# Looked-up ids broadcast by DMA as 16-bit halves, a shorter GpSimd clear between gathers, and constants built between the first gathers

## The reference, cut to what matters

```python
e = jnp.stack([tbl_0[ids[:, 0]], tbl_1[ids[:, 1]], ..., tbl_38[ids[:, 38]]], axis=1)   # (512, 39, 32)
p = e[:, ROW, :]                                  # ROW, COL: all i < j
q = e[:, COL, :]
z = jnp.einsum('bpc,apc,bpa->bp', p, w, q)        # (512, 741)
h = jnp.concatenate([z, dense_ctx], axis=1)       # (512, 757)
h = jnp.maximum(h @ W_top1 + b_top1, 0.0)         # 512 wide
h = jnp.maximum(h @ W_top2 + b_top2, 0.0)         # 256 wide
y = h @ W_top3
```

## Time and profile before

| | us |
|---|---|
| median of 3 runs | 199.92 (199.55 to 202.13) |
| profiled execution, own time | 198.71 |
| its span | 197.0 |
| TensorE matmul busy | 184.5 (94%) |
| VectorE busy | 144.1 (73%) |
| GpSimd busy | 135.4 (69%) |
| ScalarE busy | 42.7 (22%) |

### The profile page before, as it was taken

The page is one execution under the profiler, slowest core; times in us unless marked ns, Lnnn a source line. Parts: engine busy times, 40 slices in busy tenths (PEclk is TensorE's granted clock), DMA queues, the critical chain, the costliest instruction groups (busy, mean ns, idle before and its releaser), DMA issues.

```text
span 197.0 us, 3278 instructions
## 1 busy us (share of the span) xinstructions
PE 184.5 (94%) x1320; PEld 64.4 (33%) x1320; DVE 144.1 (73%) x137; ACT 42.7 (22%) x64; POOL 135.4 (69%) x202
## 2 busy tenths in 40 slices
PE   6999988969999999999999999799989976999895
PEld 3534533332222222322322222223322212222782
DVE  4889998965899989976663999589664349747600
ACT  4956941030001100111112100110121111210722
POOL 7988899888888888888888888888922200440000
PEclk9999999999999999999999999999999999999999
DMA  6999940000000100000000000000000000000000
GB/s 166 278 290 419 387 138 15 10 17 12 10 13 10 20 10 12 12 14 13 10 13 14 11 13 10 15 13 15 12 0 3 0 0 0 0 5 0 0 0 0
DMA packets 6688, 9.75 MB, mean 49 GB/s; under 512 B 1977, under 2 KB 4477, under 8 KB 6673
## 3 DMA queue, kind: packets, MB, share of 16 engines
q1 hardware_dynamic: 3696, 8.00, 12.6%
q0 software_dynamic: 2944, 1.51, 4.4%
q10 hardware_dynamic: 32, 0.03, 0.1%
HBM read 9.53 MB, written 0.00 MB: 48 GB/s over the span
## 4 chain that ended last, share of the span: by engine, by line
POOL 55%; PE 32%; issue 7%; DVE 2%; DMA 1%; ACT 1%; DVEq 0%; POOLq 0%
POOL gathered L395 41%; POOL pause L402 13%; PE ps L609 10%; PE ps L623 10%; PE ps L634 6%; PE ps L654 4%; PE ps L646 2%; DVE prod L518 2%; DMA gathered<-tbl,ids_sb 1%; POOL sel L384 1%; PE ps L587 1%; PE ps L663 0%; ACT eT L448 0%; POOL sel L387 0%; ACT z_sb L455 0%
## 5 line engine op out<-in xcount | busy, mean ns | idle before, releaser
L518 DVE TENSOR_TENSOR prod<-ps,eT 128x1024 f32<-128x1024 f32 (+2 forms) x91 | 110.2, 1265 | 36.2 <-PE ps L609 31.6
L395 POOL DMA_INDIRECT gathered<-tbl,ids_sb x92 | 92.3, 1003 | 15.2 <-issue 15.0
L609 PE MATMUL ps<-eT,w_sb 32*128 32x512 f32 (+2 forms) x380 | 70.7, 640 | 4.4 <-DVE prod L518 2.9
L623 PE MATMUL ps<-prod,sel 128*32 128x512 f32 x380 | 51.5, 604 | 0.0
L609 PEld LDWEIGHTS ps<-eT,w_sb 32*128 32x128 f32 (+2 forms) x380 | 22.0, 183 | 52.0 <-issue 25.1
L402 POOL MEMSET pause<- 128x256 f32 x91 | 30.3, 333 | 0.1
L503 DVE TENSOR_SCALAR hot<-ids_half,row_of 125x2048 bf16<-125x2048 f16 x34 | 27.8, 881 | 1.5 <-PE ps L576 0.9
L409 POOL TENSOR_TENSOR tabs<-tabs 128x512 f32<-128x512 f32 x8 | 10.1, 1264 | 25.0 <-ACT tabs L469 25.0
L576 PE MATMUL ps<-hot,lower 125*32 125x512 bf16 x272 | 22.0, 401 | 0.0
L634 PE MATMUL ps<-z_sb,w_sb 128*128 128x512 f32 x40 | 20.4, 624 | 0.7 <-ACT eT L448 0.7
L623 PEld LDWEIGHTS ps<-prod,sel 128*32 128x32 f32 x380 | 8.1, 108 | 33.7 <-issue 21.0
(11 more groups left out here) (36 smaller groups left out, 63.5 us busy)
## 6 DMA issues: line engine op xcount, KB each, us to landing
w_sb<-w SPq DMA_DIRECT2D x1, 1536.0 KB
gathered<-tbl,ids_sb POOLq DMA_INDIRECT x92, 2.3
tabs<-hot SPq DMA_DIRECT2D x3, 448.0 KB
w_sb<-wst SPq DMA_DIRECT2D x1, 640.0 KB, 13.1
w_sb<-wst SPq DMA_DIRECT2D x1, 576.0 KB, 12.0
tabs<-hot SPq DMA_DIRECT2D x1, 560.0 KB
w_sb<-wst SPq DMA_DIRECT2D x1, 512.0 KB, 10.5
w_sb<-w SPq DMA_DIRECT2D x1, 512.0 KB
```

The source lines that it names most:

```text
L395: pool.indirect_dma_start(gathered[J][:, b, K * r:K * r + K], None, tables[f], bass.IndirectOffsetOnAxis(ap=ids_sb[:, F * b + f:F * b + f ...
L518: dve.tensor_tensor(prod[:, x:x + n, :], ps[:, s:s + n, :], eT[:, I:I + 1, :].broadcast_to([P, n, B]), ALU.mult).then_inc(multiplied, 1)
L609: mm = pe.matmul(ps[:, RUN_BANK[p] + i - first, :], w_sb[rows, w_tile(q), :], eT[rows, J, :], start=True, stop=True)
L623: mm = pe.matmul(z_ps[K * (u % G):K * (u % G) + K, :], sel[:, u // G, :], prod[:, RUN_SLOT[p] + t - FIRST_TILE[p], :], start=(u < G), stop ...
```

## The change

**The ids** of the looked-up fields are handed over as 16-bit integers, one row of 2048 for each group. Four DMAs with a repeated source row bring them straight to 125 partitions: group 0 from ScalarE's queue as its first instruction, groups 1, 2 and 3 from SyncE's queue, each ahead of table 1, of table 2, and of the pair matrices of block 0. Everything of the old way goes: the int32 load, the f16 cast, `spread`, the 16 products, the copies from PSUM. `ids_half` is now unsigned 16-bit.

**GpSimd** makes the row numbers, waits for the ids and issues its first gather. The five steps that make the identity and `sel` stand behind gathers 1 to 5 in place of clears; from the sixth on the clear is 128x128.

**TensorE** starts with 14 products of zeros of 128x128x512 in bf16 on bank 7, and none later. The look-ups have banks of their own (4 and 5 for group 2).

**ScalarE** makes the lower tables of group 0 in two pieces of four slices, and TensorE waits for each piece. In the plan "lower" 1, 2 and 3 stand behind the look-ups of the group before; each still stands ahead of that group's "keep" on ScalarE.

```diff
-PAUSE = 256
-WARM = [2, 2]
+PAUSE = 128
+WARM = 14
+LOWER_PIECES = [[(0, 4), (4, 8)], [(0, 8)], [(0, 8)], [(0, 10)]]
...
-    steps += [("ids", 0), ("lower", 0), ("ids", 1), ("hot", 0, 0, 8), ("look", 0, 0, 3), ("lower", 1), ("ids", 2),
-              ("look", 0, 3, 8), ("keep", 0), ("lower", 2), ("ids", 3), ("hot", 1, 0, 8), ("look", 1, 0, 8),
-              ("lower", 3), ("keep", 1), ("hot", 2, 0, 8), ("look", 2, 0, 8), ("keep", 2), ("hot", 3, 0, 4),
+    steps += [("lower", 0), ("hot", 0, 0, 8), ("look", 0, 0, 8), ("lower", 1), ("keep", 0), ("hot", 1, 0, 8),
+              ("look", 1, 0, 8), ("lower", 2), ("keep", 1), ("hot", 2, 0, 8), ("look", 2, 0, 8), ("lower", 3),
+              ("keep", 2), ("hot", 3, 0, 4),
...
-        ids_half = [sb(f"ids_half{h}", [P, G, B], F16) for h in range(NHOT)]
+        ids_half = [sb(f"ids_half{h}", [P, G, B], U16) for h in range(NHOT)]
...
-        look_ps = [[ps[:, bank, :] for bank in banks] for banks in [(0, 1), (2, 3), (0, 1), (6, 7)]]
-        ids_ps = [ps[0:HP, bank:bank + G, :] for bank in (0, 4, 4, 4)]
+        look_ps = [[ps[:, bank, :] for bank in banks] for banks in [(0, 1), (2, 3), (4, 5), (6, 7)]]
...
+            def load_hot_ids(h):
+                sp.dma_start(ids_half[h][0:HP, :, :].rearrange("p f b -> p (f b)"),
+                             hot_ids[h:h + 1, :].broadcast_to([HP, G * B])).then_inc(hot_ids_in[h], 16)
+
             sp.dma_start(ids_sb[:, :], ids).then_inc(ids_in, 16)
             load_table(0)
+            load_hot_ids(1)
             load_table(1)
+            load_hot_ids(2)
             load_table(2)
+            load_hot_ids(3)
             for J in range(3):
                 load_w(J)
             load_table(3)
...
-            pauses = 0
+            gathers = pauses = 0
...
-                    if pauses:
-                        pool.wait_ge(paused, pauses)
-                    if (J, r, b) != (*fields[-1], NCHUNK - 1):
+                    gathers += 1
+
+                    if gathers == 1:
+                        pool.memset(ident[:, :], 0.0).then_inc(consts_zero, 1)
+                    elif gathers == 2:
+                        pool.wait_ge(consts_zero, 1)
+                        pool.affine_select(out=ident[:, :], in_=ident[:, :], compare_op=ALU.not_equal, fill=1.0,
+                                           base=0, pattern=[[-1, P]], channel_multiplier=1).then_inc(consts_made, 1)
+                    elif gathers == 3:
+                        pool.memset(sel[:, :, :], 1.0).then_inc(consts_zero, 1)
+                    elif gathers == 4:
...
+                    elif gathers < NCHUNK * len(fields):
+                        if pauses:
+                            pool.wait_ge(paused, pauses)
                         pool.memset(pause[:, :], 0.0).then_inc(paused, 1)
                         pauses += 1
...
-            act.dma_start(hot_ids_sb[:, :], hot_ids).then_inc(hot_ids_in, 16)
-            act.wait_ge(hot_ids_in, 16)
-            act.activation(ids16[:, :], hot_ids_sb[:, :], ACT.Copy).then_inc(ids16_made, 1)
+            act.dma_start(ids_half[0][0:HP, :, :].rearrange("p f b -> p (f b)"),
+                          hot_ids[0:1, :].broadcast_to([HP, G * B])).then_inc(hot_ids_in[0], 16)
...
                     act.wait_ge(tab_in[h], 16 * len(tab_pieces))
-                    for i in range(2):
-                        act.activation(lower[i][h][0:HP, :, :], bytes_of[h][0:HP, :, 1 - i::4], ACT.Copy,
-                                       scale=256.0 if i == 0 else 1.0).then_inc(lower_made, 1)
+                    for a, b in LOWER_PIECES[h]:
+                        for i in range(2):
+                            act.activation(lower[i][h][0:HP, :, K * a:K * b],
+                                           bytes_of[h][0:HP, :, 4 * K * a + 1 - i:4 * K * b:4], ACT.Copy,
+                                           scale=256.0 if i == 0 else 1.0).then_inc(lower_made, 1)
...
-            dve.memset(prod[0:K, 0, :], 0.0).then_inc(warm_zeroed, 1)
-            dve.wait_ge(consts_made, 1)
-            dve.tensor_copy(spread[:, :, :], ident[0:NHOT * G, 0:NHOT * G].rearrange("p (f o) -> p f o", o=1)
-                            .broadcast_to([NHOT * G, NHOT * G, HP])).then_inc(spread_made, 1)
+            dve.memset(prod[:, 0, :], 0.0).then_inc(warm_zeroed, 1)
...
-            keep_warm(2, WARM[0])
-            pe.wait_ge(ids16_made, 1)
-            pe.wait_ge(spread_made, 1)
+            zeros = prod[:, 0, :].bitcast(BF16)
+            for _ in range(WARM):
+                pe.matmul(ps[:, 7, :], zeros[:, 0:P], zeros[:, 0:B], start=True, stop=True)
...
-                        pe.wait_ge(lower_made, 2 * (h + 1))
-                        if h == 2:
-                            pe.wait_ge(eT_made, turns(LOOKED[0]))
                     for c in range(c0, c1):
                         n = SLICE_BASE[h] + c
+                        if any(c == a for a, _ in LOWER_PIECES[h]):
+                            pe.wait_ge(lower_made, lowers_of(h, c))
                         pe.wait_ge(hot_made, n + 1)
...
-    arrays["hot_ids"] = np.ascontiguousarray(a["ids"].T[[f for fields in HOT_FIELDS for f in fields]])
+    arrays["hot_ids"] = np.ascontiguousarray(np.ascontiguousarray(a["ids"].T).view(np.uint16)[:, ::2]
+                                             [[f for fields in HOT_FIELDS for f in fields]].reshape(NHOT, -1))
```

More of the change, by code:

```diff
@@ L10 @@
 BF16 = mybir.dt.bfloat16
-F16 = mybir.dt.float16
 F32 = mybir.dt.float32
@@ L207, in turns, with lowers_of @@
     return TURNS.index(J) + 1
-def halves_of(h):
-    return h + 2
+def lowers_of(h, c):
+    return 2 * (sum(len(pieces) for pieces in LOWER_PIECES[:h]) + 1 + [a <= c < b for a, b in LOWER_PIECES[h]].index(True))
 def lay_out_weights(w, W_top1):
@@ L286, in dlrm_tower @@
         ids_in = sem("ids_in")
-        hot_ids_in = sem("hot_ids_in")
+        hot_ids_in = [sem(f"hot_ids_in{h}") for h in range(NHOT)]
         tab_in = [sem(f"tab_in{h}") for h in range(NHOT)]
@@ L420, in _ @@
             for step in PLAN:
-                if step[0] == "ids":
-                    h = step[1]
-                    if h == 0:
-                        for part in (slice(0, 2), slice(3, 4)):
-                            act.wait_ge(ids_spread, part.stop)
-                            act.activation(ids_half[h][0:HP, part, :], ids_ps[h][:, part, :],
-                                           ACT.Copy).then_inc(ids_half_made, 1)
-                    else:
-                        act.wait_ge(ids_spread, G * (h + 1))
-                        act.activation(ids_half[h][0:HP, :, :], ids_ps[h], ACT.Copy).then_inc(ids_half_made, 1)
-                elif step[0] == "lower":
+                if step[0] == "lower":
                     h = step[1]
                     act.wait_ge(tab_in[h], 16 * len(tab_pieces))
-                    for i in range(2):
-                        act.activation(lower[i][h][0:HP, :, :], bytes_of[h][0:HP, :, 1 - i::4], ACT.Copy,
-                                       scale=256.0 if i == 0 else 1.0).then_inc(lower_made, 1)
+                    for a, b in LOWER_PIECES[h]:
[3 more added lines that the diff above has]
+                                           scale=256.0 if i == 0 else 1.0).then_inc(lower_made, 1)
                 elif step[0] == "keep":
@@ L461, in _ @@
                         act.wait_ge(mlp_in, 16 * len(mlp_loads))
-                        act.wait_ge(lower_made, 2 * NHOT)
+                        act.wait_ge(lower_made, lowers_of(NHOT - 1, NSLICE[-1] - 1))
                         act.wait_ge(hot_used, len(hot_block))
@@ L536, in side_free @@
                     pe.wait_ge(*side_used.pop())
-            def keep_warm(bank, n):
-                zeros = prod[0:K, 0, :]
-                for _ in range(n):
-                    pe.matmul(ps[:, bank, 0:B // 2], zeros[:, 0:P], zeros[:, 0:B // 2], start=True, stop=True)
             pe.wait_ge(warm_zeroed, 1)
-            keep_warm(2, WARM[0])
-            pe.wait_ge(ids16_made, 1)
-            pe.wait_ge(spread_made, 1)
+            zeros = prod[:, 0, :].bitcast(BF16)
+            for _ in range(WARM):
+                pe.matmul(ps[:, 7, :], zeros[:, 0:P], zeros[:, 0:B], start=True, stop=True)
             for step in PLAN:
-                if step[0] == "ids":
-                    h = step[1]
-                    if h > 1:
-                        pe.wait_ge(ids_half_made, halves_of(h - 1))
-                    for r in range(G):
-                        pe.matmul(ids_ps[h][:, r, :], spread[:, G * h + r, :], ids16[:, :],
-                                  start=True, stop=True).then_inc(ids_spread, 1)
-                    if h == 1:
-                        pe.wait_ge(third_made, 1)
-                        pe.wait_ge(ids_half_made, halves_of(0))
-                        keep_warm(2, WARM[1])
-                elif step[0] == "look":
+                if step[0] == "look":
                     h, c0, c1 = step[1:]
```

33 lines of the change are left out of this document (9 added, 24 removed).

## The result

The changed kernel takes **209.28 us** (median of 4 runs, 206.87 to 209.89) where the kernel before takes 199.85 us (199.55 to 202.13): ratio 1.042, 95% interval 1.031 to 1.054. The forecast was 199.1 us, range 194.2 to 203.2. The profiled execution took 209.85 us with a span of 208.1 us, against 197.0 before.

A forecast was written before the change was run, and what follows sets the result against it. TensorE's list and the front that starts it were taken as the bound, GpSimd's gathers being worth only 1.34 us. Front shift +0.5 less 1.34 gave -0.8 us, from a median of 199.92 to 199.1 us, range 194.2 to 203.2.

The forecast's parts named there:

- The bound and the stall: TensorE's list sets the time once begun; its one wait for block 8's gathered rows goes with the shorter clear, -1.34 us.
- The comparisons: VectorE's look-up slices wait for GpSimd's clear; the shorter one gives 0.77 us a slice from 0.835, bounds 0.835 and 0.66.
- The slow form for unsigned ids: Rival, chance 0.03: unsigned 16-bit ids cost VectorE's comparisons their fast form, +15 us, 214 us.
- The ids' arrival: Group 0's ids land at 9.75 us: 1.9 plus 50 rows at 0.157 us on five DMA engines; 12.8 at 0.218.
- divisor rule: A DMA uses the largest number of engines up to 16 dividing its rows, so 125 rows run on five.
- The cold start: TensorE stands still before the look-ups and may begin them at the low clock: 0.5 us charged, bounds 0 and 2.
- At no cost ... the other groups' ids: Id loads of groups 1 and 2 land near 11.4 and 17 us at 0.157 us per row, before use, costing nothing.
- 1.9 + 141p: Landing time of table 3 behind the id broadcasts, p us per row; above p = 0.189 ScalarE's keep 2 must wait.
- The gathers' ids: Row ids for GpSimd's gathers share engines with the broadcast: 1 us later at most, covered by 6 us of slack.
- Table 3 behind the backlog: Rival, chance 0.10: table 3 lands late behind the id loads and holds up ScalarE's keep 2, +4.9, 204.8 us.
- the ids did not come early: Rival, chance 0.27, claimed early ids: group 0's at 5.5 us, first multiplication at 27.2, total -5.5, 194.4 us.
- the comparisons did gain: Rival, chance 0.10, claimed no gain: the clear does not disturb the comparisons, slices stay at 0.835 us, +1.0, 200.9 us.

The follow-up runs named there:

- experiment 2: Changed kernel with each id load going to 128 partitions: 197.51 us, ratio 0.973; with the old clear of 256 columns as well: 204.36 us, ratio 1.020.
- experiment 5: Changed kernel with id loads split 112 and 13, gathers' ids first, constants before the gathers: 196.39 us with clear 128, 199.79 us with clear 256.
- experiment 3(b): Changed kernel with only group 0's id load on 128 partitions, the others at 125: 294.26 us on a chip where VectorE is held up; table 3 lands at 35.5.

## Why the prediction was wrong, step by step

- **The bound and the stall.** Right that a shift of the first multiplication passes through to the end, to 0.1 us in the table above, and GpSimd's period past 45 us is 1.33 us (1.32 forecast). That the wait for block 8's rows is gone is in part luck. Its last gather starts 2.9 us earlier and not some 8, since the first gather is 1.6 us later and the clears beside the comparisons grew; the rows land near 122.7 us (120.28 + 2.4), not by 119. TensorE did not wait because its own front was late: with the front mended and the same clear it waits twice, 1.5 us in all (experiment 2). The wait is gone where the gathers also start early, at 3.17 us (experiment 5).
- **The comparisons.** Quicker, as forecast, but by a wrong mechanism. I took the comparison to wait for the clear, and 0.77 us a slice; 22 slices took 15.49 us, 0.704 each, inside the bound of 0.66. The slow form for unsigned ids is out with it. It is the clear that waits, as the groups of 14 to 26 us show (count, busy us and mean ns, idle before), and then all clears with min/median/max in ns:

```profile
L494 DVE TENSOR_SCALAR hot<-ids_half,row_of 125x2048 bf16<-125x2048 uint16 x19 | 13.1, 765 | 0.0
...
L408 POOL MEMSET pause<- 128x128 f32 x6 | 4.0, 671 | 0.0
```

```profile
L408 POOL MEMSET pause<- x86: 218/219/696, 15.1 to 135.9; 128x128 f32 x86
```

  Before, one comparison in two stretched to 1.12 us beside a clear of 0.326; now none does, and the clear takes 0.671 us instead of 0.218. GpSimd's period there is 2.03 us, where 1.202 + 0.205 + 0.165 would be 1.57. It cost nothing here; in experiment 2 it and the late first gather together leave the 1.5 us of waits. The Trainium skill's page "SBUF — State Buffer" (section "Who interferes with whom") says that the shared port pair is an exclusive lock and that issue order decides who blocks; these rows agree.
- **The ids' arrival.** 10.96 us against 9.75. The five engines fit: 128 rows or a split bring 6.0 to 6.4 us, and from 10.5 to 11.0 us the DMA share is 0.32, where five of sixteen are 0.31. The row cost (10.96 - 1.9) / 50 = 0.181 us, between my 0.157 and 0.218. I chose the fast end on the ground that eleven engines soon run out of such rows. They run out only about when the ids arrive: the mean share is 1.00 from 8 to 9 us, 0.79 from 9 to 10 and 0.45 from 10 to 12. The divisor rule that the prediction cites from the Trainium skill, page "DMA: Bandwidth & Descriptors" (section "Why a DMA increments its semaphore by 16 and not by 1"), agrees with these numbers.
- **The cold start.** Forecast 0.5 us. The slices ran at half pace from 12.3 to about 17 us, and table 0, which I had landing near 4.5 us, was there at 11.0 and held the look-ups until 12.3. Group 2's look-ups end near 31.7 us, 2.3 later than forecast. The last thing to hold them up was the lower part of table 2, made at 26.38 us, when TensorE had been free for 1.25 us; the other 1 us comes from the ids and these two. The prediction called the half pace of the earlier trace rows the 1.2 GHz level. In the changed kernel the same pace, 1.28 us a slice, has a granted clock of 0.50 beside it; in the kernel before the granted clock reads 1.00 from 8 to 14 us, so there the level is not shown.
- **"At no cost ... the other groups' ids". This is the step that failed.** I asked only whether each load would be there when used, and gave each row 0.157 us. What three broadcasts on five engines do to the loads behind them was left to a rival with a chance of 0.10. They made table 2 land at 24.4 us and table 3 at 34.4. In its formula 1.9 + 141p, the landing at 34.4 us means p = 0.23, above the upper bound that I had read from a stretch where all engines shared the load. SyncE comes to a stand too, 7.28 us for three issues that took 1.30 before, so that table 3 is not issued until 14.34 us; experiment 3(b), with 7.57 us, puts that down to the later groups. It need not have cost anything: group 3's ids, ahead of table 3 in the same queue and issued by 6.68 us, landed only at 30.56 us in the second execution of the changed kernel, and table 3 3.8 us behind them:

```profile
30.56 2.92 DVE L494 TENSOR_SCALAR hot<-ids_half,row_of 125x2048 bf16<-125x2048 uint16 x4 [1.78 <-DMA ids_half<-hot_ids]
```

- **The gathers' ids.** "1 us later at most": they landed in 4.5 us instead of 2.2. It cost nothing while the front was later still; with the front mended it was what ended the chain (experiment 2).
- **The rival.** "Table 3 behind the backlog" named the right transfer, the right waiting instruction and the right side, at 204.8 us. It came out at 209.3 because of p and of the low clock behind the standstill (2.0 us in one execution, 0.7 us in another), which neither it nor the forecast had priced. A chance of 0.10 was too small: its threshold, p above 0.189, lay in the middle of my two rows, 0.157 and 0.218. Of the other rivals, the ids did not come early, and the comparisons did gain.

## What to carry to other kernels

The broadcasts to 125 partitions, on five DMA engines as far as the numbers tell, made everything behind them late: table 3 landed at 34.4 us and by 22.6 with 128 rows. Give such a load 128 rows, or split it, and cost the loads behind it and not only itself. Before a computation is replaced by a transfer, ask when the transfer ends in the queue as it stands; here the ids came at 10.96 us, where TensorE had made them by 6.32, and no earlier than 6.0 when the loads were mended. When two engines set the end by turns, write the time as a sum of both, because mending one shows what the other costs.

## What the runs showed that was not expected

- The pause between gathers, which looks like idle work, decides on some chips how much VectorE gets to run: 218, 237 and 279 us with clears of 512, 256 and 128 columns on one chip, and on another 196.4 us with the shorter clear and 199.8 with the longer in the version of experiment 5. The Trainium skill's page "SBUF — State Buffer" (section "Who interferes with whom") has a VectorE instruction with one SBUF input, outside the 2-port modes, free of the lock; the held-up multiplications read one tile in PSUM and one in SBUF, and no run tells what holds them.
- One kernel's time differs by up to 26% from chip to chip (199.9 to 252.4 us), far more than any edit here is worth on a good one.
- TensorE's granted clock fell for some 3 us near 175 us in one execution of the changed kernel and near 163 us in one of the version with 128 rows, and not in a second execution of the changed kernel, whose idle times before that point are the same kind. What set it off stays open.
